# First stage of an attention and mixture-of-experts layer: VectorE's routing chains run step by step in turn, slots allotted one batch later, token counts in a value bank

## The reference

```python
xn = _layernorm(x, axis=-1)
x = x + _L0_attn_ref(xn, ...) + _L0_ffn_ref(xn, ...)
# attention: 16 heads of 16, causal window of 128
q = (x @ Wq.T + bq); k = (x @ Wk.T + bk); v = (x @ Wv.T + bv)
# experts: 8 of them, 512 wide, two for each token, and a shared one
logits = xt @ gate_w.T
_, idx = jax.lax.top_k(logits + beta, K)
probs = jax.nn.sigmoid(jnp.take_along_axis(logits, idx, axis=-1))
```

## Time and profile before

| | |
|---|---|
| median of 3 runs | 1661.37 us (1656.77 to 1661.45) |
| the profiled execution | 1655.14 us |
| its span in the profile | 1653.4 us |
| busy in the span | PE 1520.1, PEld 1252.6, DVE 1105.7, ACT 979.6, POOL 1109.0 us |
| first stage | from 0 to about 240 us |

### The profile page before, as it was taken

The page is one execution under the profiler, slowest core; times in us unless marked ns, Lnnn a source line. Parts: engine busy times, 40 slices in busy tenths (PEclk is TensorE's granted clock), DMA queues, the critical chain, the costliest instruction groups (busy, mean ns, idle before and its releaser), DMA issues.

```text
span 1653.4 us, 38959 instructions
## 1 busy us (share of the span) xinstructions
PE 1520.1 (92%) x11382; PEld 1252.6 (76%) x11382; DVE 1105.7 (67%) x3788; ACT 979.6 (59%) x2043; POOL 1109.0 (67%) x1158
## 2 busy tenths in 40 slices
PE   4878868999999999999998899999999999999998
PEld 4766747998888999888997666677777777667766
DVE  7999875666666666666666566766666676666652
ACT  5767744454455455544554466666666666666664
POOL 1878775334433444434331488999999999999998
PEclk9999988999999999999999599999999999999999
DMA  6777755554555555545576477878877777788752
GB/s 195 269 269 269 286 195 184 170 165 156 162 165 168 160 170 164 162 138 176 164 245 149 89 155 159 178 167 174 172 173 163 163 155 164 165 168 176 168 133 88
DMA packets 228581, 288.89 MB, mean 175 GB/s; under 512 B 59488, under 2 KB 146144, under 8 KB 228512
## 3 DMA queue, kind: packets, MB, share of 16 engines
q1 hardware_dynamic: 170064, 207.30, 46.9%
q10 hardware_dynamic: 45488, 45.36, 9.6%
q0 software_dynamic: 12960, 35.41, 8.5%
HBM read 198.07 MB, written 79.95 MB: 168 GB/s over the span
## 4 chain that ended last, share of the span: by engine, by line
PE 58%; DVE 15%; ACT 10%; issue 8%; ACTq 4%; POOL 3%; DMA 2%; DVEq 0%; POOLq 0%
PE psum L152 33%; PE psum L970 11%; PE psum L1573 5%; PE psum L1531 4%; ACT plain_arena L1688 4%; PE psum L1554 2%; DVE split_arena L736 2%; PE psum L1157 2%; DVE plain_arena L1804 2%; ACTq L1707 1%; DVE stats L631 1%; ACTq L1708 1%; DVE split_arena L729 1%; ACT plain_arena L1702 1%; ACT plain_arena L1749 1%
## 5 line engine op out<-in xcount | busy, mean ns | idle before, releaser
L152 PE MATMUL psum<-split_arena 128*128 128x512 f32 (+2 forms) x4752 | 939.0, 350 | 12.3 <-DVE split_arena L1261 7.3
L152 PEld LDWEIGHTS psum<-split_arena 128*128 128x128 f32 x4752 | 750.3, 192 | 132.6 <-issue 22.9
L1804 DVE CUSTOM_DVE_ANT_0 plain_arena<-psum,mask 128x256 f32<-128x256 f32 (+1 forms) x1024 | 338.4, 385 | 198.0 <-PE psum L1531 194.2
L1688 ACT ACTIVATE plain_arena<-psum 128x512 f32<-128x512 f32 (+1 forms) x512 | 250.3, 541 | 201.7 <-PE psum L1554 171.9
L1120 POOL TENSOR_TENSOR split_arena<-plain_arena,split_arena 128x1024 fp32r<-128x1024 f32 x43 | 103.2, 2401 | 227.3 <-ACT split_arena L1192 227.0
L1226 ACT ACTIVATE plain_arena<-psum 128x512 f32<-128x512 f32 (+1 forms) x172 | 90.2, 525 | 249.7 <-PE psum L152 249.6
L970 PE MATMUL psum<-split_arena 128*128 128x256 f32 x1704 | 217.9, 286 | 3.5 <-DVE split_arena L1291 3.5
L970 PEld LDWEIGHTS psum<-split_arena 128*128 128x128 f32 x1704 | 208.0, 191 | 5.7 <-DVE split_arena L1291 4.1
L1296 DVE TENSOR_TENSOR plain_arena<-psum,plain_arena 128x512 f32<-128x512 f32 (+1 forms) x172 | 102.3, 595 | 139.9 <-ACT plain_arena L1226 137.6
L1112 POOL DMA_INDIRECT plain_arena<-xn_d,run_ix x142 | 137.1, 965 | 69.2 <-POOL run_ix L1109 35.2
L1448 POOL TENSOR_SCALAR_AFFINE_SELECT plain_arena<-plain_arena 128x1024 f32<-128x1024 f32 x128 | 140.5, 1098 | 39.5 <-ACT plain_arena L1688 38.7
(11 more groups left out here) (199 smaller groups left out, 1852.7 us busy)
## 6 DMA issues: line engine op xcount, KB each, us to landing
plain_arena<-in_gate_w SPq DMA_DIRECT2D x43, 512.0 KB, 3.4
plain_arena<-in_up_w SPq DMA_DIRECT2D x43, 512.0 KB, 4.1
plain_arena<-in_down_w SPq DMA_DIRECT2D x43, 512.0 KB, 3.4
plain_arena<-in_x SPq DMA_DIRECT2D x32, 512.0 KB, 7.0
q_d<-split_arena SPq DMA_DIRECT2D x32, 512.0 KB, 3.6
k_d<-split_arena SPq DMA_DIRECT2D x32, 512.0 KB, 5.1
split_arena<-q_d SPq DMA_DIRECT2D x128, 128.0 KB, 4.4
split_arena<-k_d SPq DMA_DIRECT2D x128, 128.0 KB, 4.8
```

The costliest lines, as they stand in the source:

```text
L152: last = pe.matmul(out, lhs_t(p), rhs(q), start=(begins and c == 0 and k == 0), stop=(ends and c == len(chunks) - 1 and k == 2), skip_grou ...
L1688: act.activation(b_pt[:, g % 2, 2 * p + par, 4 * half:4 * half + n, :].rearrange("p k s -> p (k s)"), psum[:, 2 + par, 0:n * P], ACT.Exp, ...
L1804: last = dve.tensor_tensor_reduce(b_junk[:, 2 * par + i % 2, 0:cols], psum[:, par, at:at + cols], mask[:, 2 * P - cols:2 * P], -1.0, 3e38, ...
```

## The change

Each of DVE's chains becomes a function of a step number, and turn t calls them in alternation: step n of `choose(t-1)`, step n of `allot(t-2)`, and from n = 8 on a step of `inverse_root`. The wait for the step before stays, ahead of each step. `allot` now handles the batch before the one it handled, so `top` gets two halves; its product has a tile of its own (`apart_at`). The splitting of slot numbers goes from POOL to DVE: four steps at the end of `allot` in place of six on POOL. On PE `prefix` stands between the value tiles 1 and 2, and `tokens_to_slots` behind tile 3 writes to columns 264 to 419 of bank 6, for which it waits until ACT has copied value tile 2. `turn_rows` no longer waits for `token_places`; `values_and_logits` does. In the last two turns `allot(15)` follows alone, `rank_blocks` and `proj_lo(15)` move.

```diff
-                then(pool.tensor_copy(slot_at[:, :], flat))
-                then(pool.tensor_scalar(slot_pc[:, 1, :], slot_at[:, :], 1.0 / P, 0.5 * (1 - P) / P, ALU.mult, ALU.add))
...
                 for n in range(2 * T):
-                    last = pool.tensor_scalar(in_row[:, v, n, :], steps_f[:, 0:P], slot_pc[:, 0, n:n + 1], None, ALU.is_equal)
+                    last = pool.tensor_scalar(in_row[:, v, n, :], steps_f[:, 0:P], slot_pc[:, v, n:n + 1], None, ALU.is_equal)
...
+                elif n == RT:
+                    dve.tensor_copy(slot[:, ds(b * T, T), :], slot_f[:, :, :])
+                    dve.tensor_scalar(slot_at[:, :], flat, 1.0 / P, 0.5 * (1 - P) / P, ALU.mult, ALU.add).then_inc(p_ps, 1)
+                elif n == RT + 1:
+                    dve.wait_ge(p_ps, PS * b + 1)
+                    dve.tensor_scalar(slot_at[:, :], slot_at[:, :], ROUND, None, ALU.add).then_inc(p_ps, 1)
+                elif n == RT + 2:
+                    dve.wait_ge(p_ps, PS * b + 2)
+                    if b >= 2:
+                        dve.wait_ge(p_oh, b - 1)
+                        dve.wait_ge(p_ch, (2 * T - MARKED) * (b - 1))
+                    dve.tensor_scalar(col_at[:, v, :], slot_at[:, :], -ROUND, None, ALU.add).then_inc(p_ps, 1)
+                elif n == RT + 3:
+                    dve.wait_ge(p_ps, PS * b + 3)
+                    dve.scalar_tensor_tensor(out=slot_pc[:, v, :], in0=col_at[:, v, :], scalar=-float(P), in1=flat,
+                                             op0=ALU.mult, op1=ALU.add).then_inc(p_ps, 1)
...
-                    last = pe.matmul(psum[:, 1, 0:NC], in_row[:, v, n, :], in_col[:, v, n, :],
+                    last = pe.matmul(psum[:, 6, L:L + NC], in_row[:, v, n, :], in_col[:, v, n, :],
...
                     values_and_logits(b, u, (0, 1))
                     if done_b is not None:
                         prefix(done_b)
+                    values_and_logits(b, u, (2, 3))
+                    if listed_b is not None:
+                        pe.wait_ge(p_vb, T * t + 3)
+                        tokens_to_slots(listed_b, listed_u % 2)
...
+                g = begins_group(t)
+                if g is not None:
+                    variance(g)
+                for n in range(STEPS):
+                    if done[0] is not None:
+                        choose(done[0], done[1], n)
+                    if old[0] is not None and t <= B:
+                        allot(old[0], old[1], n)
+                    if g is not None and 0 <= n - 8 < 6:
+                        inverse_root(g, n - 8)
```

More of the change, by code:

```diff
@@ L432, in queries_or_keys, with values_and_logits @@
                          lambda part, c=c: p_xt[:, v, part, c, :]) for c in range(KD)]).then_inc(p_mm, 1)
-            def values_and_logits(b, v):
-                pe.wait_ge(p_xlo, b + 1)
-                for a in range(T):
+            def values_and_logits(b, v, tiles):
+                if tiles[0] == 0:
+                    pe.wait_ge(p_xlo, b + 1)
+                    after(pe, p_or, b - 2)
+                for a in tiles:
                     after(pe, p_vb, T * b + a - 1)
@@ L699, in allot @@
+            def allot(b, u, n):
+                v = u % 2
                 wide = lambda row: row[:, :].unsqueeze(1).to_broadcast([P, T, E])
@@ L707, in allot @@
-                dve.tensor_tensor(newest[:, :], upto, need[:, :], ALU.mult)
-                then(dve.tensor_tensor(start[:, :], upto, need[:, :], ALU.subtract))
-                then(dve.scalar_tensor_tensor(out=offset[:, :], in0=start[:, :], scalar=float(BLK), in1=behind[:, :],
-                                              op0=ALU.mult, op1=ALU.subtract))
-                then(dve.scalar_tensor_tensor(out=shift[:, :, :], in0=place[:, :, :], scalar=0.0, in1=wide(offset),
-                                              op0=ALU.is_ge, op1=ALU.mult))
@@ L874, in turn @@
                     statistics(*ahead)
-                if begins_group(t) is not None:
-                    variance(begins_group(t))
-                if done[0] is not None:
-                    choose(done[0], done[1])
-                if begins_group(t) is not None:
-                    inverse_root(begins_group(t))
-                if isinstance(t, int) and t == -2:
+                g = begins_group(t)
[8 more added lines that the diff above has]
+                        inverse_root(g, n - 8)
+                if t == -2:
                     first_state()
@@ L885, in turn @@
                     rows_lo(next_[0], next_[1])
-                if isinstance(t, int) and t == B:
-                    allot(done[0])
+                if t == B:
+                    for n in range(STEPS):
+                        allot(done[0], done[1], n)
+                    block_use()
                 if t == B + 1:
@@ L899, in turn @@
                     proj_lo(old[0], old[1], 1)
-                if done[0] is not None and not (isinstance(t, int) and t == B):
-                    allot(done[0])
                 if t == B:
-                    block_use()
                     token_places(old[0])
-                elif t >= 3:
+                elif 3 <= t < B:
                     token_places(t - 3)
```

194 lines of the change are left out of this document (102 added, 92 removed).

## The result

The changed kernel takes 1640.56 us in the median of four runs (1638.74 to 1642.39), the kernel before 1661.41 (1656.77 to 1665.05): ratio 0.988, interval 0.986 to 0.990. That is 20.9 us faster, clear of the scatter; forecast were 24.4, to 1637.

What follows compares the result with a forecast made beforehand. DVE was taken to bound the steady turns, POOL the last ones. Gains 3.9 + 10 x 2.07 + 2.8 less 3.2 make 24.2 us: 1655.1 to 1631 profiled, 1637 against the median 1661.4; range 1627 to 1646.

Steps and rivals of the forecast that it cites:

- the first term: On DVE, `choose`, `allot` and four splitting steps, alternated, take 3.6 us together instead of 6.8 one after the other.
- the rival without overlap: Small DVE instructions hold the engine until finished, so alternation hides nothing: 13.65 us a mean turn, 1673 us; chance 0.05.
- The root's own saving: In DVE's odd turns, alternated `inverse_root` adds 0.4 us instead of 1.76, with about 0.6 more for waiting on ACT.
- The loop between ACT and PE: Transposes to tile 1 copy, copies and marked columns, then normalisation: 10.90 us a turn, the next bound once DVE shortens.
- The 0.3 us added for stretched instructions: Allowance on the steady turn, taking it from the ideal 10.90 us to 11.2.
- ten turns: Steady turns 3 to 12, each 2.07 us shorter, from 13.27 to 11.2.
- PE's own sum: PE's projections, transposes, values, tokens and counts in a turn, together 9.8 us, below the loop.
- ramp: Start-up before turn 3: turn 1 loses `allot` and alternates the root, so turn 3 starts 3.9 us earlier.
- turns 13 and 14: The two turns after the steady ones, 25.11 us before, at 11.15 each now, giving 2.8 us.
- tail: From turn 15's start to the first gather: slots come a turn later, 36.7 us for 33.57, a loss of 3.2.
- the case with DMA: DMA transfers stretch the steady turn to 12.2 us if their share holds only 0.85: time 1647 us; chance 0.15.

Runs made afterwards that it cites:

- first profile: The changed kernel as it is, profiled the first time, against the kernel before: 1640.56 us, ratio 0.988, first gather at 219.39.
- second profile: The changed kernel run once more with nothing altered: 1634.85 us, ratio 0.986 to the kernel before, first gather at 217.79.

## Why the prediction was right

**The bound.** DVE's chains bound the steady turns, and the time lay between their steps: shown. With the chains one after another the gain is gone (1.003).

**The alternation.** 3.6 us were forecast for `choose` with `allot` in an even turn and 4.0 with the root. In turns 4 to 12 the even ones took 4.0 to 4.4 us, 4.2 in the mean, and the odd ones 3.9 to 4.3; only turn 16 came near, with 3.75 (194.90 to 198.65). So the first term was 0.6 us too low, which did no harm because DVE had ceased to be the bound, and the root adds nothing that can be seen. One by one the chains took 6.5 and 7.7 us, so the rival without overlap is refuted. Its price was too high as well: it has 11.5 us more than the kernel before, and the chains one by one took 2.4 more (1661.67 for 1659.29).

The Trainium skill, VectorE: DVE Perf Modes, section The DRAIN you can't avoid, has the next operation wait until the pipeline is empty. The same section adds that an operation which isn't held starts earlier. The rows agree with that addition and not with the rule from which the prediction made a rival: starts of independent steps stand 0.06 to 0.14 us apart at durations of 0.14 to 0.23, starts of dependent ones 0.22 to 0.24.

The root's own saving was mis-sized: behind the other chains it costs 1.2 us, not 1.76, and an odd turn gets half a microsecond longer.

**The loop between ACT and PE**, 5.39 + 3.44 + 2.07 = 10.90 us: measured 5.36 + 3.45 + 2.07 and a period of 10.93. The turn in the mean was forecast at 11.2 and is 11.27, so near partly by luck. The 0.3 us added for stretched instructions are not what fills the gap. Counted at PE's transposes, the ten turns take 110.77 us (49.18 to 159.95), 11.08 each: nine of them 10.9 to 11.1, and one 12.0, for the three more instructions. DVE's own cut gives more because its turn 3 took 12.85 us (44.28 to 57.13): DVE began it ahead of the loop and waited in it, 1.21 us of that for ACT's root. Neither was in the working.

**PE's own sum** was put at 9.8 us. That is too low: from 115.16 to 126.09 PE stands still for 0.44 us alone, so its own work is 10.5, and with six columns on POOL a turn without any wait takes 10.3. The loop lies only some 0.4 us above PE's work, and PE's waits before the transposes fell to 0.4 to 0.6 us (one to 1.5), not to 0.8.

**The sum**, term by term, first profile: ramp 4.6 (forecast 3.9), ten turns 20.0 (20.7), turns 13 and 14 2.2 (2.8), tail -5.9 (-3.2): 20.8 us at the first gather for 24.2. In the second profile, with the higher clock in turn 1, the ramp is 5.7. The tail is the term that was mis-sized: 39.5 us, where the working has 36.7. About half of it, 1.5, is the end: the forecast took over 5.3 us from POOL's last mark to the gather, and they were 6.8. It had the path wrong there. In both kernels the gather hangs not on that mark but on PE's order: tokens of batch 14, queries, run list and half of the keys of batch 15, last tokens. The queries became 1.23 us longer, at a granted clock of 0.54 for 0.74; the forecast named a low clock and gave it no time. The rest is 0.8 for DVE's way to the first slots (4.37 us for 3.6) and 0.6 between POOL's marks of batch 13 and its first of batch 14 (5.4 for 4.8); these were read from the trace and not tested. The experiments show what the path consists of: fewer marks give 3.0, the list ahead with the tokens before the keys 1.5.

The prediction also contradicts itself on its range: the range ends at 1646, but the case with DMA, for which it wants room, is put at 1647 and the high end at 1651.

**The other rival**, DMA as the limit: its share rose to 0.92 as worked out, and the turn stayed at 11.27. No wait of DVE for loaded rows is seen in these turns of the first profile, and one of 0.27 us in the second (at 89.22). Between the profiled run's 16.4 us of gain and the 20.8 at the gather stand the later stages, 1417.6 us for 1413.2; the second profile had 1411.8.

## What to carry to other kernels

Short dependent steps left DVE half empty here while its busy share said 92%: compare the distance of two dependent starts with that of two independent ones, and if it is double, interleave chains of different batches. A wait for another engine in one chain halts the others too (1.21 us in turn 3), so a step with such a wait belongs late. Then work out the next loop, and each engine's own sum, before counting the gain, since here DVE's mean need fell by more than the turn could. Delaying a step by a batch was paid in the tail, where the order of every engine's last pieces and the granted clock count; read the gain of such an edit at the end of its stage, not in a total that scatters by more.

## What the runs showed of the hardware

The granted clock of turn 1 was 0.78 in one profile and 1.00 in another of the same kernel; the transposes there took 1.97 us at 29.66 in the first and 1.10 at 29.02 in the second, and turn 3 started 1.1 us later. The first gather inherits that. Over the twelve profiles of the changed kernel and its variants the two go together: in six the granted clock of that window (25.90 to 33.60) was 1.00, and turn 3 started at 43.17 to 43.20; in the other six it was 0.78, and turn 3 started at 43.91 to 45.15. Before these transposes PE had stood idle for 2.44 us in both profiles; why the clock differs stays open.

With six columns, where the DMA share is 0.94 and turns fall to 10.3 us, DVE waits for loaded rows, by 0.2 us (at 65.72 and at 87.60); in the changed kernel it has no such wait from turn 3 to turn 15 in the first profile and one of 0.27 us in the second. The loads seem to be close behind ACT, PE and DVE as the next bound; no run tests it.

Single small instructions of DVE take 0.3 to 0.4 us instead of 0.17 here and there (0.37 for L628 at 136.61). Of 402 instructions with up to 32 elements in and out between 57 and 180 us, where the DMA share is 0.90, 34 took over 0.27 us; of 48 between 194 and 202, where it is 0.00, one did. In the second profile it was 3 of 44 in such a stretch (193 to 201, 0.00), so it isn't shown that DMA makes the difference. What stretches them was not tried and stays open.
